# Masked-attention graph layers in fp32: two transposing products for the cross scores become one, in the first and third of three phases

## The reference

```python
u = einsum('bid,bjd->bij', h, h) / sqrt(384)          # scores of a graph's nodes with each other
attn = softmax(u) * adjacency;  attn /= attn.sum(-1) + 1e-10
hl, hs, hr = h @ Wl.T + bl, h @ Ws.T + bs, h @ Wr.T + br
ctx = (attn * upper) @ hl + diag(attn)[..., None] * hs + (attn * lower) @ hr
o = relu(layernorm(ctx) * gamma + beta)               # eps 1e-12
```

## Time and profile before

| | |
|---|---|
| median of 3 runs | 1234.78 us (1233.87 to 1236.38) |
| the profiled execution's own time | 1234.55 us |
| its span (first to last instruction) | 1232.8 us |
| TensorE matmuls busy | 1215.1 us, 99% |
| VectorE busy | 1089.1 us, 88% |
| ScalarE busy | 833.8 us, 68% |
| GpSimd busy | 323.5 us, 26% |
| mean granted TensorE clock | 0.997 |

### The profile page before, as it was taken

How to read it: one execution, slowest core, us unless ns; L and a number is a source line. 1 busy time by engine, 2 the same in 40 slices (tenths; PEclk the granted TensorE clock), 3 DMA queues, 4 the chain that set the end, 5 groups by cost and what they waited for, 6 DMA issues and landing times.

```text
span 1232.8 us, 27495 instructions
## 1 busy us (share of the span) xinstructions
PE 1215.1 (99%) x7163; PEld 1208.2 (98%) x7163; DVE 1089.1 (88%) x3125; ACT 833.8 (68%) x2079; POOL 323.5 (26%) x438
## 2 busy tenths in 40 slices
PE   8999999999999999999999999999999999999997
PEld 7899999999999999999999999999999999999997
DVE  7888888888887889999999999999999999999986
ACT  6666666666767776666667676676666666666763
POOL 2322222222222221212112121342323232323221
PEclk9999999999999999999999999999999999999999
DMA  5433333333233333232323333432332323232331
GB/s 187 127 109 94 107 96 101 101 92 110 88 106 122 102 109 107 96 106 84 105 94 99 103 96 106 144 98 95 96 106 96 106 96 106 96 101 95 97 96 43
DMA packets 112899, 126.91 MB, mean 103 GB/s; under 512 B 11104, under 2 KB 100192, under 8 KB 112864
## 3 DMA queue, kind: packets, MB, share of 16 engines
q1 hardware_dynamic: 112864, 126.50, 32.9%
HBM read 76.91 MB, written 49.55 MB: 103 GB/s over the span
## 4 chain that ended last, share of the span: by engine, by line
PE 91%; DVE 3%; issue 3%; POOL 1%; DMA 1%; ACT 0%; SPq 0%; POOLq 0%; DVEq 0%; ACTq 0%
PE left_bank L447 23%; PE right_bank L447 23%; PE context_bank L447 23%; PE context_bank L478 16%; PE score_bank L422 5%; PE score_bank L430 1%; DMA rows<-weights 1%; DVE node_t L747 1%; DVE context L861 0%; POOL weight L1021 0%; DVE turned L743 0%; DVE in_stats L726 0%; DVE context L852 0%; DVE side_parts L828 0%; DVE score L764 0%
## 5 line engine op out<-in xcount | busy, mean ns | idle before, releaser
L447 PE MATMUL left_bank<-weight,node_t 128*128 128x384 f32 x1728 | 337.9, 338 | 0.0
L447 PE MATMUL context_bank<-weight,node_t 128*128 128x384 f32 x1728 | 332.7, 337 | 3.2 <-ACT context_bank L615 3.2
L447 PE MATMUL right_bank<-weight,node_t 128*128 128x384 f32 x1728 | 333.7, 338 | 1.0 <-ACT right_bank L603 0.6
L609 ACT ACTIVATE side_parts<-right_bank 128x384 fp32r<-128x384 f32 x192 | 94.4, 492 | 316.6 <-PE context_bank L478 316.6
L447 PEld LDWEIGHTS context_bank<-weight,node_t 128*128 128x128 f32 x1728 | 303.5, 189 | 3.7 <-ACT context_bank L615 3.5
L447 PEld LDWEIGHTS left_bank<-weight,node_t 128*128 128x128 f32 x1728 | 303.9, 188 | 0.0
L447 PEld LDWEIGHTS right_bank<-weight,node_t 128*128 128x128 f32 x1728 | 298.9, 188 | 2.1 <-issue 1.8
L478 PE MATMUL context_bank<-side_parts,attn_t 128*128 128x386 f32 x1152 | 240.7, 344 | 3.7 <-issue 3.4
L478 PEld LDWEIGHTS context_bank<-side_parts,attn_t 128*128 128x128 f32 x1152 | 199.0, 190 | 6.6 <-issue 5.7
L747 DVE TENSOR_TENSOR node_t<-nodes,node_t 128x768 fp32r<-128x768 f32 x94 | 119.8, 1275 | 18.1 <-ACT node_t L557 18.1
L1004 POOL TENSOR_TENSOR rstd<-spread,scalars 128x2 f32<-128x2 f32 x96 | 66.2, 689 | 257.6 <-DVE spread L844 257.6
(11 more groups left out here) (75 smaller groups left out, 1520.5 us busy)
## 6 DMA issues: line engine op xcount, KB each, us to landing
squares<-turned SPq DMA_DIRECT2D x94, 384.0 KB, 2.7
nodes<-squares SPq DMA_DIRECT2D x376, 96.0 KB, 2.2
rows<-x SPq DMA_DIRECT2D x64, 384.0 KB, 3.7
out<-rows SPq DMA_DIRECT2D x31, 384.0 KB, 2.6
adj_in<-adj SPq DMA_DIRECT2D x96, 64.0 KB, 1.9
piece<-weights SPq DMA_DIRECT2D x18, 192.0 KB, 2.6
rows<-weights SPq DMA_DIRECT2D x3, 576.0 KB, 7.8
vector_rows<-vectors SPq DMA_DIRECT2D x3, 384.0 KB, 7.0
```

The lines of the kernel that those rows point to most:

```text
L447: mm = nc.tensor.matmul(bank[:, 0:D], node_t[:, s.parity, k, c, a], weight[:, s.phase % 2, w, c, b], start=False, stop=(c, a) == (CH - 1, ...
L609: nc.scalar.activation(side_parts[:, side, HI, 0:D], side_bank[side][k][:, 0:D], ACT.Copy).then_inc(side_hi[side], 1)
```

## The change

In the steps of the first and the third phase the cross scores of both tiles are packed into one 128 x 128 square before they are turned. `cross` has four blocks of 64 columns. ScalarE now writes with four instructions. Two (one for each half of the partitions) copy the diagonal blocks of both tiles to where they belong. Two more copy one block each into the other half of the partitions, into the place that the square of the blocks 1 and 2 has free. TensorE turns this square with one product into columns 384 to 511 of `edge_bank`, and no longer onto `score_bank`. VectorE's two sums now wait only for the copies (`cross_packed`) and stand ahead of the statistics of later tiles. A third instruction of 128 x 128, `add_cross`, adds the turned square where the sums stood, and the exponentials wait for it. The middle phase keeps its order of work.

```diff
+        cross_blocks = cross[:, :, :].rearrange("p a (b j) -> p (a b) j", b=2)
+        cross_pack = cross_blocks[:, 1:3].rearrange("p b j -> p (b j)")
+        cross_here = [cross_blocks[half, 1 - h:4 - h:2] for h, half in enumerate(HALVES)]
+        turned_cross = edge_bank[:, 3 * P:4 * P].rearrange("p (k j) -> p k j", k=2)
...
             def transpose_first(s):
                 at_least(pe, score_summed, 2 * s.n)
+                at_least(pe, cross_added, s.n)
...
             def turn_cross(s):
 
-                pe.wait_ge(cross_copied, s.n + 1)
-                for k in range(2):
-                    mm = nc.tensor.matmul(score_bank[:, k * 256:k * 256 + P], cross[:, k], ident_r[:, :],
-                                          start=False, stop=True, skip_group_check=True)
-                mm.then_inc(cross_turned, 1)
+                if not s.bounded:
...
+                    return
+                pe.wait_ge(cross_packed, 4 * (s.normal + 1))
+                at_least(pe, cross_added, s.normal)
+                nc.tensor.matmul(edge_bank[:, 3 * P:4 * P], cross_pack, ident_r[:, :],
+                                 start=True, stop=True, skip_group_check=True).then_inc(cross_turned, 1)
...
             def copy_cross(s):
                 act.wait_ge(scored, s.n + 1)
...
+                at_least(act, cross_turned, s.n)
                 at_least(act, score_summed, 2 * s.n)
-                nc.scalar.activation(cross[:, :, :], scores4[:, :, 1, :], ACT.Copy).then_inc(cross_copied, 1)
+                for h, half in enumerate(HALVES):
+                    nc.scalar.activation(cross_here[h], scores4[half, :, 1, half], ACT.Copy).then_inc(cross_packed, 1)
+                for h, half in enumerate(HALVES):
+                    nc.scalar.activation(cross_blocks[HALVES[1 - h], 1 + h], scores4[half, 1 - h, 1, half], ACT.Copy).then_inc(cross_packed, 1)
...
-                act.wait_ge(score_summed, 2 * s.n + 2)
+                act.wait_ge(cross_added, s.normal + 1)
...
             def sum_scores(s):
...
+                dve.wait_ge(cross_packed, 4 * (s.normal + 1))
+                for h, half in enumerate(HALVES):
+                    nc.vector.tensor_tensor(score[half], scores4[half, :, 0, half], cross_here[h].bitcast(F32),
+                                            ALU.add).then_inc(score_summed, 1)
+
+            def add_cross(s):
+
                 dve.wait_ge(cross_turned, s.n + 1)
...
+                dve.wait_ge(score_summed, 2 * s.n + 2)
+                nc.vector.tensor_tensor(score[:, :, :], score[:, :, :], turned_cross, ALU.add).then_inc(cross_added, 1)
...
                     centre(prev, 1)
+                if nxt.exists() and nxt.bounded:
+                    sum_scores(nxt)
                 if fourth.exists() and fourth.bounded:
                     input_stats(fourth, 0)
                     input_stats(fourth, 1)
                 if prev.exists():
                     norm(prev, 0)
-                if nxt.exists():
+                if nxt.exists() and nxt.bounded:
+                    add_cross(nxt)
+                elif nxt.exists():
                     sum_scores(nxt)
```

More of the change, by code:

```diff
@@ L236, in adj_gnn_program @@
         cross_copied = sem("cross_copied")
+        cross_packed = sem("cross_packed")
         cross_turned = sem("cross_turned")
+        cross_added = sem("cross_added")
         score_summed = sem("score_summed")
@@ L426, in turn_cross @@
             def turn_cross(s):
-                pe.wait_ge(cross_copied, s.n + 1)
-                for k in range(2):
-                    mm = nc.tensor.matmul(score_bank[:, k * 256:k * 256 + P], cross[:, k], ident_r[:, :],
-                                          start=False, stop=True, skip_group_check=True)
-                mm.then_inc(cross_turned, 1)
+                if not s.bounded:
+                    pe.wait_ge(cross_copied, s.n + 1 - PAIRS)
+                    for k in range(2):
+                        mm = nc.tensor.matmul(score_bank[:, k * 256:k * 256 + P], cross[:, k], ident_r[:, :],
+                                              start=False, stop=True, skip_group_check=True)
+                    mm.then_inc(cross_turned, 1)
+                    return
[3 more added lines that the diff above has]
+                                 start=True, stop=True, skip_group_check=True).then_inc(cross_turned, 1)
             def spread_max(s):
@@ L566, in copy_cross @@
                 act.wait_ge(scored, s.n + 1)
+                if not s.bounded:
+                    at_least(act, score_summed, 2 * s.n)
+                    nc.scalar.activation(cross[:, :, :], scores4[:, :, 1, :], ACT.Copy).then_inc(cross_copied, 1)
+                    return
+                at_least(act, cross_turned, s.n)
                 at_least(act, score_summed, 2 * s.n)
-                nc.scalar.activation(cross[:, :, :], scores4[:, :, 1, :], ACT.Copy).then_inc(cross_copied, 1)
+                for h, half in enumerate(HALVES):
+                    nc.scalar.activation(cross_here[h], scores4[half, :, 1, half], ACT.Copy).then_inc(cross_packed, 1)
+                for h, half in enumerate(HALVES):
+                    nc.scalar.activation(cross_blocks[HALVES[1 - h], 1 + h], scores4[half, 1 - h, 1, half], ACT.Copy).then_inc(cross_packed, 1)
             def totals(s):
@@ L760, in sum_scores @@
             def sum_scores(s):
+                if not s.bounded:
+                    dve.wait_ge(cross_turned, s.n + 1)
+                    for h, half in enumerate(HALVES):
+                        nc.vector.tensor_tensor(score[half], scores4[half, :, 0, h * NODES:(h + 1) * NODES],
+                                                cross[half, :, h * NODES:(h + 1) * NODES].bitcast(F32),
+                                                ALU.add).then_inc(score_summed, 1)
+                    return
+                dve.wait_ge(cross_packed, 4 * (s.normal + 1))
+                for h, half in enumerate(HALVES):
+                    nc.vector.tensor_tensor(score[half], scores4[half, :, 0, half], cross_here[h].bitcast(F32),
+                                            ALU.add).then_inc(score_summed, 1)
+            def add_cross(s):
                 dve.wait_ge(cross_turned, s.n + 1)
[L763 to L766, removed]
+                dve.wait_ge(score_summed, 2 * s.n + 2)
+                nc.vector.tensor_tensor(score[:, :, :], score[:, :, :], turned_cross, ALU.add).then_inc(cross_added, 1)
             def row_maximum(s):
@@ L881, in first_step @@
                 sum_scores(s)
+                add_cross(s)
                 split_side(s, 0, LEFT)
```

## The result

| | before | after |
|---|---|---|
| median | 1235.51 us (1233.87 to 1236.83, 6 runs) | 1240.80 us (1239.91 to 1243.03, 6 runs) |
| ratio | | 1.0046, 95% interval 1.0035 to 1.0058 |
| the profiled execution | 1234.55 us, span 1232.8 | 1241.70 us, span 1239.9 |
| step in the loop of the first phase | 12.467 us | 12.347 us |
| middle phase | 12.593 | 12.593 |

What follows compares the result with a forecast made beforehand. TensorE was taken to bound the first phase, TensorE and a loop through VectorE and ScalarE together the third. - 3.8 - 0.5 + 0.1 + 7.3 = + 3.1 on 1234.55 gave 1237.7, predicted as 1238.0 us; range 1232.5 to 1250.

Steps and rivals of the forecast that it cites:

- TensorE, 0.12 a step (3.8 us): First phase, 32 steps: one 128 x 128 product less saves 0.12 us per step, 3.8 us.
- The 0.5 for the last steps: Last 4 steps of the third phase, without statistics of later tiles: the saved product earns 0.5 us.
- TensorE and the loop tie in the third phase: Third phase: loop VectorE, TensorE's weighing, ScalarE, VectorE is as long as TensorE's work or 0.02 us longer, 12.49 a step.
- Rival A: Whole kernel: TensorE alone binds, all 64 turns earn 0.12, 1227.1 us; chance 0.09 together with smaller gains.
- VectorE, 0.25 a step for `add_cross`: VectorE: the added instruction costs 0.25 us in each of 29 steps, mostly third phase, 7.3 us (4.9 to 10.4).
- rival B: VectorE: gaps between partition halves shrink, 0.18 a step instead of 0.25, total 1235.8 us, no change; chance 0.25.
- ScalarE, late sums 0: Four copies on ScalarE overlap and end 0.70 us after the first starts, so VectorE's moved sums wait 0.
- rival C: ScalarE's four copies do not overlap, take 1.08, sums start 0.38 late, 1251.5 us; chance 0.16.
- C's other half: First phase: TensorE's load of the square comes 0.08 us late or more, taking back most of the 3.8.
- The start, + 0.1: Step 0, where the turn follows the copy closely: TensorE loses about 0.1 us, once.
- The sum: Whole kernel: - 3.8 - 0.5 + 0.1 + 7.3 = + 3.1 us on the profiled execution.
- What I had named as the test: Profile after: first-phase step 12.35 us, third about 12.74, weighing of tile 1 at 1.3 or more, sums at most 0.1 after `centre`.

Runs made afterwards that it cites:

- e3: Changed kernel, but steps 0 and 1 keep the old form and the counts are moved by two; 1242.81 us, ratio 1.0065 to the kernel before.
- e9: Kernel before, with VectorE's residual of tile 1 moved ahead of the next step's transpose in the third phase, its store one step later; 1234.77 us, ratio 0.9998.
- e12: e8 with the middle phase also counting `cross_packed` and `cross_added`, so third-phase waits follow the step number; 1227.52 us, ratio 0.9941 to the kernel before.
- e5: Changed kernel with the four copies over all 128 partitions, two into an unused tile (turned square holds wrong blocks); 1234.17 us, ratio 0.9989 to the kernel before.
- e10: Changed kernel with ScalarE's four copies ordered by the half they read; 1240.95 us, ratio 1.0043 to the kernel before.
- e6: Kernel before plus one unused VectorE instruction of `add_cross`'s shape behind the sums in the third phase; 1234.41 us, ratio 0.9992.
- e8: Changed kernel with sums directly ahead of `add_cross`, third-phase residual of tile 1 later, steps 0 and 1 in old form; 1229.87 us, ratio 0.9953 to the kernel before.

## Why the prediction was right, and where it was not

- **TensorE, 0.12 a step (3.8 us).** Right: 12.467 to 12.347, in all kernels that pack in the first phase but e3, whose moved counts cost 0.08. It was read from a difference of steps in two phases, not from the product's own 0.22 to 0.25 us. The 0.5 for the last steps was 0.3 to 0.5.
- **TensorE and the loop tie in the third phase.** Right (e9: 12.467 with the loop relieved). This decided the sign. Rival A's rule, that the busiest engine is the bound, would have given 1227.1 us. That is about what e12 has, but only with the loop opened by hand.
- **VectorE, 0.25 a step for `add_cross`.** Too much: 0.10 (e5). Its 0.29 was right, the following instruction came after 0.21, and the gaps moved as rival B said: 0.03 less behind the second sum, 0.11 more ahead of `add_cross`, 0.11 less ahead of the low part. B's 0.18 was itself high: it did not count that the first gathering (L731) began 0.07 behind the start of a memset before, while it (L752) now follows `add_cross` directly. Why L870 came 0.32 behind L785 in the middle phase, on which the 0.25 leaned, no run settles.
- **ScalarE, late sums 0.** The step that failed. The prediction let the four copies overlap by 0.1 each, took 0.70, and set the wait of the sums at nothing. They do not overlap, need 1.06, and the sums come 0.25 late. That is rival C's mechanism, and nearly C's own 1.08. C's 0.38 assumed that VectorE starts 0.13 behind the last copy; it starts 0.03 behind it, 0.10 less. C's other half, that the first phase's gain is taken back, did not happen: the fourth copy ends 0.25 ahead of the product, its weights load 0.07 after it, and the step is 12.347. One slip in the prediction had no effect: its second line for the copies, through 0.49 and 0.39, gives 0.76 and not 0.1 less than 0.78. With overlap they do take 0.68 (e5).
- **The start, + 0.1.** Too little: about 2 us.
- **The sum.** 0.10 + 0.25 = 0.35 a step were lost on VectorE, 0.33 of it shown in the step, where the prediction had 0.25 + 0. Against + 3.1 on the profiled execution stand + 7.1 there and + 5.3 on the medians. The prediction counted 29 steps that pay; 26 looped ones paid 0.33, and the passage into the phase 0.2 in all. The verdict, slower, rests on the tie, which holds. That the size came out inside the range was partly luck: an instruction taken as too dear stood in for a wait taken as absent. The range was also said to take in most of C, but its end of 1250 lies below C's own 1251.5.
- **What I had named as the test.** TensorE 12.35: seen. Third phase about 12.74: 12.82. Weighing of tile 1 at 1.3 or more: 1.40. "Wrong if the sums start more than 0.1 after `centre` is done": they start 0.15 to 0.17 after it, and that was C.

## What to carry to other kernels

Where the busiest engine and a loop through two others have the same length, an instruction saved on the first pays only where the loop has room; measure the room in each phase before moving work, and open the loop first. Four partial copies in place of one cost their full lengths, without overlap, if each changes the partitions it starts in, and the price is paid by whoever waits for the last one. A semaphore that is counted in step with the loop's own number saves the wait value's extra register instruction, which was worth 0.08 us a step here.

## What the runs showed of the hardware

- ScalarE gives up its overlap when the half of the partitions changes between neighbours. Copies of 128 columns on all partitions start 0.17 apart (e5), on changing halves 0.30 (the changed kernel); of 64 columns 0.10 and 0.24. A change on the read side alone and one on the written side alone both did it (e10). A copy of 64 partitions without a change overlapped its neighbour by 0.10 (step 0 of the changed kernel).
- VectorE does the same, and the gap follows the next reader of PSUM, not only the next instruction. An instruction of 0.29 us put where it absorbs the gap was free (e6, 9.19 us against 9.21).
- A register instruction that carries a wait, ahead of a product on TensorE, delayed the weight load from 0.07 to 0.12 us after the last copy, and cost 0.08 us a step (e12 against e8). With the copies 0.38 earlier the product was not followed late (e5).
